# Graph layers on one core: the first chunk's turned tiles parked on chip, and five single operations moved

## The chip, the cores and the metric

One core of a Trainium2 chip runs the whole program. The metric is the device time of one execution in microseconds (us), from launch to end. Engines are named as in the profile: PE (TensorE, matmuls), DVE (VectorE), ACT (ScalarE), POOL (GpSimd), SP (SyncE). DMA queues are named by the engine that issues into them.

## The reference, cut to what matters

`adj` is 4096 x 4096 in float32 (sparse, random weights), `x` is 4096 x 128. Four layers run one after another; each is `x = layernorm(x + layer(x))`:

```python
# layer 0: two products with adj
out = adj @ (sum(d_list * filt * d_list)[:, None] * (adj @ (x @ weight))) + bias
# layer 1: A' = a * A, with (1 - a) added on the diagonal
out = relu((A' @ x) / rowsum(A') [:, None] @ W.T + b)
# layer 2: lap_mul(A, x) = d * (A @ (d * x)), d = 1 / sqrt(rowsum(A))
z = leaky_relu(lap_mul(A, x) @ W1 + b1, 0.1)
S = exp(-sqrt(max(|z_i - z_j|^2, 0) + 1e-10) / 2), kept for the 4 nearest j of each row, else 0
out = lap_mul(S + A, x) @ W2 + b2
# layer 3
out = relu(concat([x, A @ x]) @ W.T + b)
```

The program needs five products with `adj`. Every one goes over all of `adj`, so the transposed matrix is made once and read again.

## The kernel before

**Pass 0.** `adj` comes in 8 chunks of 512 rows. SP loads a chunk in 512-column units into four `nat` buffers in `region`. For each of the chunk's 32 tiles (`kt`) PE transposes four 128 x 128 blocks into `pt` (L1330). ACT writes the high fp16 part of the turned tile (`split_high`, L671), DVE the low part (L1082), and both also sum rows (L682, L1094). Between the transposes PE does three matmuls (L1310, L1312, L1314) of the tile four earlier; every fp32-like product is three fp16 matmuls. While it does chunk 0, DVE builds the operand `yop` as well (L1041).

Tiles `kt < 7` (KEPT) of every chunk stay on chip, in `kept[c]`. The other 25 tiles of a chunk form 5 units of 5. A unit is written into one of two stages, alternately (`s = (5 * c + u) % 2`), and POOL writes the stage to `at_scratch` in HBM in two parts, of 3 and 2 tiles, 768 and 512 KB (`store_units`, L506). ACT may overwrite a stage's part only when its last store has landed (`stage_stored`), which is two units later. One queue, POOL's, carries these stores in the order in which they are issued; SP's queue carries the loads. Chunks 0 and 1 are written out in the program, the later ones run in a loop, in which a nop stands ahead of each store to hold the wait.

**Passes 1 to 3** read the units back (SP, `early_slot` first) and use the kept tiles from chip.

**Near phase** (layer 2's neighbours). For each of 32 blocks of rows `i`, PE makes 128 x 4096 closeness values in eight PSUM banks (L1419 to L1426; four by `first_banks`, four by `second_banks`). ACT copies the banks to `region` (L718), DVE finds the largest (MAX8, L1145) and their places (L1146). `PROJECTION_AT` places the steps of another small task in this stream: each `projection_step(k)` is, on PE, a projection of group k-1 (L1238) and a turn of group k (L1209), on ACT the two copies behind them. Key 2i-1 puts a step between the banks of row i, key 2i behind them. After every fourth row come POOL's distances and degree sums, ACT's Sqrt and Exp (`weights`), ACT's Sqrt of the degrees (L742), and DVE's `inverse(g)` (reciprocal L1151, product with a constant L1152), whose results feed POOL's `scales` and ACT's `high_y`.

**Pass 4** follows with 128 gathers by POOL (L605). **Pass 5** starts while layer 2's last part (`mix`, layernorm, `yop` at L880) is still running on DVE: it takes units u = 0 to 4 in turn, and `KEPT5[u]` are the kept columns, which are ready early, that PE does before unit u. The last chunk of pass 5 is done in two halves of 256 rows: `sums_half` on ACT, `project_half` on PE (into `late_nat`), `last_half` on DVE, the output store by ACT.

Of the kernel before, what the change touches and what calls it, by code (L numbers as in the profile page):

```python
# [25 lines left out]
ALU = mybir.AluOpType  # L26
# [14 lines left out]
X_PARTS = 8  # L41
TOP = 4
# [13 lines left out]
PROJECTION_AT = {1: 1, 2: 2, 4: 3, 5: 4, 7: 5, 8: 6, 10: 7, 11: 8}  # L56
# [23 lines left out]
def gnn_kernel(nc, x, adj, d_list, w0, filt, bias0, alpha, w1, b1, wz, bz, w2, b2, w3, b3, out):  # L80
# [19 lines left out]
    with ExitStack() as ctx:  # L100
# [10 lines left out]
        kept = sb("kept", [P, NCH, KEPT, 2, CHUNK], F16)  # L111
        slot_elems = UNIT * 2 * CHUNK
# [134 lines left out]
        stage_used = sem("stage_used")  # L247
# [137 lines left out]
        def _(sp):  # L385
# [20 lines left out]
            def early_slot(u):  # L406
# [6 lines left out]
                if u == UPC - 1:  # L413
                    sp.wait_ge(acc_full, NCH)
                for s in range(2):
                    units = NCH * UPC // 2 if u >= UPC - 2 + s else (UPC + 1 - s) // 2
                    for part in range(len(STORES)):
                        sp.wait_ge(stage_stored[s][part], 16 * units)
# [66 lines left out]
        def _(pool):  # L485
# [13 lines left out]
            def store_units(c, par, m):  # L499
                for u in range(UPC):  # L500
                    s = (par * UPC + u) % 2
                    for part, (k0, k1) in enumerate(STORES):
                        pool.wait_ge(low_done, c * KT + KEPT + u * UNIT + k1)
                        pool.nop(nofuse=True)
                        cols = slice(k0 * 2 * CHUNK, k1 * 2 * CHUNK)
                        pool.dma_start(at_dram[bass.ds(c, 1), u, :, cols].rearrange("c p n -> (c p) n"),  # L506
                                       stage_flat[s][:, cols]).then_inc(stage_stored[s][part], 16)
            each_chunk(pool, store_units)
# [77 lines left out]
            def scales(g_tiles, g):  # L586
                nc.gpsimd.tensor_tensor(S[:, g_tiles, :], S[:, g_tiles, :], dinv2y[:, g_tiles].unsqueeze(2)
# [59 lines left out]
        def _(act):  # L647
# [5 lines left out]
            def split_high(c, par, m):  # L653
                for kt in range(KT):
                    g = c * KT + kt
                    act.wait_ge(tr_done, g + 1)
                    if kt < KEPT:
                        dst = kept[:, bass.ds(c, 1), kt, 0, :].rearrange("p c n -> p (c n)")
                    else:
                        u = (kt - KEPT) // UNIT  # L660
                        s = (par * UPC + u) % 2
                        if (kt - KEPT) % UNIT == 0 and not (isinstance(c, int) and c * UPC + u < 2):
# [4 lines left out]
                        for part, (k0, k1) in enumerate(STORES):  # L667
                            if (kt - KEPT) % UNIT == k0 and not (isinstance(c, int) and c * UPC + u < 2):
                                act.wait_ge(stage_stored[s][part], 16 * (m * UPC + (par * UPC + u) // 2))
# [25 lines left out]
            each_chunk(act, split_high, 4)  # L695
# [36 lines left out]
            def weights(g):  # L732
# [4 lines left out]
                nc.scalar.activation(S[:, tiles_g, :], S[:, tiles_g, :], ACT.Exp, scale=-0.5).then_inc(S_ready, 1)  # L737

# [36 lines left out]
            projection_step(0)  # L775
# [75 lines left out]
        def _(dve):  # L851
# [158 lines left out]
            def last_half(h):  # L1010
# [7 lines left out]
                dve.wait_ge(x3_loaded[(NCH - 1) % X3_BUFFERS], 16 * ((NCH - 1) // X3_BUFFERS + 1))  # L1018
                step(nc.vector.scalar_tensor_tensor(t_nat[:, half, :], t_nat[:, half, :], 0.0,
                                                    gath[(NCH - 1) % X3_BUFFERS][:, half, :], ALU.max, ALU.add))  # L1020
# [51 lines left out]
            def split_low(c, par, m):  # L1072
                for kt in range(KT):
                    g = c * KT + kt
                    dve.wait_ge(high_done, g + 1)
                    if kt < KEPT:
                        hi = kept[:, bass.ds(c, 1), kt, 0, :].rearrange("p c n -> p (c n)")
                        lo = kept[:, bass.ds(c, 1), kt, 1, :].rearrange("p c n -> p (c n)")
                    else:
# [570 lines left out]
```

## Time and profile before

| | us |
|---|---|
| median of 3 runs | 1424.22 |
| lowest, highest | 1420.53, 1425.78 |
| the profiled execution, its own time | 1423.97 |
| its span, first to last instruction | 1422.4 |

The granted clock of PE is 0.999 of full speed over the span. The profiled execution stands 0.25 us under the median; 1.57 us of its time lie outside the span. A busy share of an engine is an average over stages: pass 0 (to about 400 us), the streaming passes (to about 840), the near phase (to about 1140), pass 4 with its gathers, and pass 5.

### The profile page before, as it was taken

Reading aid. Unit: us, or ns where it says so; the run is one execution under the profiler, and the core shown is the slowest. Engines: PE = TensorE matmul, PEld = TensorE weight load, DVE = VectorE, ACT = ScalarE, POOL = GpSimd, SP = SyncE. Lnnn points to the kernel's source line nnn. Section 1 sums busy time; section 2 is a strip of 40 time slices with the busy share of each in tenths; the row PEclk is TensorE's granted clock in tenths of the full one; section 3 lists DMA queues with packets and bytes.
Section 4 is the critical chain, followed back from the end, with each engine's and each line's share of the span. In section 5 each row is a group of like instructions: output and inputs, shape, how many; then the busy total and the mean of one; then the engine's idle time right before and its main releaser. Section 6 shows DMA issues by size and latency. Waiting matters only on the chain.

```text
span 1422.4 us, 20428 instructions
## 1 busy us (share of the span) xinstructions
PE 1385.7 (97%) x7365; PEld 794.7 (56%) x7365; DVE 849.1 (60%) x1324; ACT 452.7 (32%) x958; POOL 236.0 (17%) x356
## 2 busy tenths in 40 slices
PE   7999999999999999999999999999999999999998
PEld 6888887877544444544445445444444444444467
DVE  7877766666323433434323359999999846655144
ACT  5767665655300000000010136655555410000011
POOL 2111110110100100000000000111111167776000
PEclk9999999999999999999999999999999999999999
DMA  9999998887999879987787812203444699999863
GB/s 348 393 376 386 357 329 327 319 301 268 335 388 355 348 303 391 412 356 297 291 325 277 307 31 89 89 16 119 133 134 133 237 391 403 404 379 403 353 244 115
DMA packets 111699, 407.53 MB, mean 287 GB/s; under 512 B 11696, under 2 KB 28080, under 8 KB 90112
## 3 DMA queue, kind: packets, MB, share of 16 engines
q1 hardware_dynamic: 79520, 316.43, 59.9%
q0 software_dynamic: 19728, 73.71, 13.3%
q10 hardware_dynamic: 12368, 16.26, 3.2%
q8 instruction: 55, 0.90, 0.2%
q14 instruction: 28, 0.23, 0.0%
HBM read 339.77 MB, written 66.58 MB: 286 GB/s over the span
## 4 chain that ended last, share of the span: by engine, by line
PE 66%; DVE 19%; DMA 7%; POOL 4%; issue 2%; ACT 1%; SPq 0%; DVEq 0%; POOLq 0%; ACTq 0%
PE acc L1262 10%; PE acc L1264 10%; PE acc L1263 10%; DVE hT L1145 8%; PE pt L1330 5%; DVE wT L1146 4%; DMA region<-in_adj 4%; POOL gath_all L605 4%; DVE wz_sb L1146 3%; PE pt L1264 3%; PE pt L1262 3%; PE pt L1263 3%; PE acc L1310 3%; PE acc L1312 2%; PE acc L1314 2%
## 5 line engine op out<-in xcount | busy, mean ns | idle before, releaser
L1330 PE MATMUL pt<-ident,region 128*128 128x128 f32 x1024 | 244.0, 279 | 13.5 <-DMA region<-in_adj 12.6
L1330 PEld LDWEIGHTS pt<-ident,region 128*128 128x128 f32 x1024 | 200.4, 196 | 40.8 <-issue 7.7
L1262 PE MATMUL acc<-region,yop 128*128 128x512 f16 (+1 forms) x581 | 217.8, 375 | 4.0 <-DVE yop L880 2.7
L1264 PE MATMUL acc<-region,yop 128*128 128x512 f16 (+1 forms) x581 | 217.5, 374 | 0.0
L1263 PE MATMUL acc<-region,yop 128*128 128x512 f16 (+1 forms) x581 | 217.5, 374 | 0.0
L1082 DVE SCALAR_TENSOR_TENSOR region<-pt,region 128x512 f16<-128x512 f32 x200 | 136.2, 687 | 75.5 <-ACT region L671 74.9
L718 ACT ACTIVATE region<-pt 128x512 f32<-128x512 f32 x256 | 133.0, 603 | 114.5 <-PE pt L1426 46.4
L671 ACT ACTIVATE region<-pt 128x512 f16<-128x512 f32 x200 | 118.1, 596 | 110.1 <-PE pt L1330 99.6
L1145 DVE MAX8 hT<-region 128x8 f32<-128x4096 f32 x31 | 136.8, 4412 | 2.3 <-ACT region L718 2.3
L1419 PE MATMUL pt<-yop 128*128 128x512 f16 x256 | 97.9, 382 | 8.6 <-ACT region L718 7.5
L639 ACT ACTIVATE std<-mv,eps_ln 128x4 f32<-128x4 f32 x31 | 9.2, 297 | 280.0 <-DVE mv L889 280.0
L1420 PE MATMUL pt<-yop 128*128 128x512 f16 x256 | 97.0, 379 | 0.0
L1421 PE MATMUL pt<-yop 128*128 128x512 f16 x256 | 97.0, 379 | 0.0
L1262 PEld LDWEIGHTS acc<-region,yop 128*128 128x128 f16 x581 | 56.8, 98 | 70.6 <-issue 6.0
L1262 PE MATMUL pt<-region,yop 128*128 128x512 f16 x250 | 94.8, 379 | 1.5 <-DMA region<-at_scratch 1.5
L1263 PE MATMUL pt<-region,yop 128*128 128x512 f16 x250 | 94.8, 379 | 0.0
L1264 PE MATMUL pt<-region,yop 128*128 128x512 f16 x250 | 94.8, 379 | 0.0
L506 POOL DMA_DIRECT2D at_scratch<-region x80 | 42.6, 532 | 308.6 <-DVE region L1082 298.9
L1264 PEld LDWEIGHTS acc<-region,yop 128*128 128x128 f16 x581 | 56.9, 98 | 65.9
L1263 PEld LDWEIGHTS acc<-region,yop 128*128 128x128 f16 x581 | 56.9, 98 | 59.8
L1094 DVE TENSOR_REDUCE rs_part<-region 128x1 f32<-128x512 f32 x128 | 86.6, 676 | 0.0
L1310 PE MATMUL acc<-region,yop 128*128 128x512 f16 x200 | 75.8, 379 | 2.5 <-DVE yop L1041 2.5
(257 smaller groups left out, 2278.8 us busy)
## 6 DMA issues: line engine op xcount, KB each, us to landing
region<-at_scratch SPq DMA_DIRECT2D x163, 1280.0 KB, 8.0
region<-in_adj SPq DMA_DIRECT2D x128, 512.0 KB, 7.6
at_scratch<-region POOLq DMA_DIRECT2D x40, 768.0 KB, 6.7
at_scratch<-region POOLq DMA_DIRECT2D x40, 512.0 KB, 6.8
region<-at_scratch SPq DMA_DIRECT2D x76, 256.0 KB, 2.7
x_scratch<-xout ACTq DMA_DIRECT2D x16, 256.0 KB, 10.8
region<-at_scratch ACTq DMA_DIRECT2D x3, 1280.0 KB, 9.8
gath_all<-x_scratch POOLq DMA_DIRECT2D x12, 256.0 KB, 5.3
```

Of the source, the lines that this page charges most:

```text
L671: nc.scalar.activation(dst, pt[kt % 4][:, :], ACT.Copy, scale=A_SCALE).then_inc(high_done, 1)
L718: nc.scalar.activation(near[i % 2][:, j * CHUNK:(j + 1) * CHUNK], near_bank(i, j)[:, :], ACT.Copy).then_inc(near_copied, 1)
L1082: nc.vector.scalar_tensor_tensor(lo, pt[kt % 4][:, :], A_SCALE, hi, ALU.mult, ALU.subtract).then_inc(low_done, 1)
L1145: step(nc.vector.max(top8[:, i, :], near[i % 2]))
L1146: nc.vector.max_index(idx8(i), top8[:, i, :], near[i % 2]).then_inc(near_used, 1)
L1262: nc.tensor.matmul(into, y[:, 0, kt, :], high, start=(kt == first_tile), stop=False)
L1263: nc.tensor.matmul(into, y[:, 0, kt, :], low, start=False, stop=False)
L1264: return nc.tensor.matmul(into, y[:, 1, kt, :], high, start=False, stop=(kt == last_tile))
L1310: nc.tensor.matmul(acc[par][:, :], yh, hi, start=(kt == 0), stop=False)
L1330: ins = nc.tensor.transpose(pt[kt % 4][:, t * P:(t + 1) * P], nat[u % 4][:, t, b * BLOCK + j:(b + 1) * BLOCK:PAIR], ident[:, :])
L1419: nc.tensor.matmul(into, zh, zT[:, 0, cols], start=True, stop=False)
L1420: nc.tensor.matmul(into, zh, zT[:, 1, cols], start=False, stop=False)
```

## The change

The 25 tiles of chunk 0 that are not kept go into the kept store of chunks 4 to 7, which is empty so far (`parked`), and not into the stages. POOL writes each parked unit to HBM later, as one transfer of 128 x 5120 fp16 (1.31 MB), behind the store of another chunk's unit: `PARKED_AT` says that unit 0 goes behind unit 2 of chunk 2, unit 1 behind (3, 1), unit 2 behind (4, 1), units 3 and 4 behind (5, 0) and (5, 2). ACT waits for them at the start of chunks 4, 5 and 6 (`PARKED_BEFORE`). ACT's and POOL's loops over the chunks are written out, and the nop ahead of a store is gone. The five moves: the projection steps are placed anew, with step 0 behind row 1; the product with a constant leaves `inverse` for POOL's `scales`; ACT does a Sqrt of one column behind the last Exp; the last chunk's bias is added by a PE matmul (identity by bias, 128 x 256 in f32) and no longer by DVE, and ACT's `sums_half(1)` stands behind the first half's output; one column of KEPT5 moves from unit 4 to unit 1.

```diff
+PARKED = 4
+PARKED_AT = {(2, 2): 0, (3, 1): 1, (4, 1): 2, (5, 0): 3, (5, 2): 4}
+PARKED_BEFORE = {4: 2, 5: 3, 6: 5}
...
-PROJECTION_AT = {1: 1, 2: 2, 4: 3, 5: 4, 7: 5, 8: 6, 10: 7, 11: 8}
+PROJECTION_AT = {2: 0, 3: 1, 4: 2, 6: 3, 7: 4, 8: 5, 10: 6, 11: 7, 12: 8}
...
+        def parked(k0, k1):
+            return kept_tiles[:, PARKED * KEPT + k0 - KEPT:PARKED * KEPT + k1 - KEPT, :, :]
...
+                sp.wait_ge(parked_stored, 16 * UPC)
...
-            def store_units(c, par, m):
+            for c in range(1, NCH):
                 for u in range(UPC):
-                    s = (par * UPC + u) % 2
+                    s = (c * UPC + u) % 2
                     for part, (k0, k1) in enumerate(STORES):
                         pool.wait_ge(low_done, c * KT + KEPT + u * UNIT + k1)
-                        pool.nop(nofuse=True)
...
+                    if (c, u) in PARKED_AT:
+                        k = PARKED_AT[c, u]
+                        pool.dma_start(at_dram[0, k, :, :], parked(KEPT + k * UNIT, KEPT + (k + 1) * UNIT)
+                                       .rearrange("p k h n -> p (k h n)")).then_inc(parked_stored, 16)
...
+                step(nc.gpsimd.tensor_scalar(dinv2y[:, g_tiles], dinv2[:, g_tiles], 1.0 / Y_SCALE[3], None, ALU.mult))
...
+                    if kt == 0 and c in PARKED_BEFORE:
+                        act.wait_ge(parked_stored, 16 * PARKED_BEFORE[c])
...
+                    elif c == 0:
+                        dst = parked(kt, kt + 1)[:, 0, 0, :]
...
-            each_chunk(act, split_high, 4)
+            for c in range(NCH):
+                split_high(c, c % 2, c // 2)
...
+                if g == NCH - 1:
+                    nc.scalar.activation(std[:, 0:1], eps_ln[:, 0:1], ACT.Sqrt)
...
-            sums_half(1)
             for h in range(2):
                 half = slice(h * TPC // 2, (h + 1) * TPC // 2)
+                if h == 1:
+                    sums_half(1)
...
-                nc.vector.tensor_tensor(t_nat[:, half, :], late_nat[:, half, :], bias[5][:, :].unsqueeze(1).to_broadcast([P, TPC // 2, D]),
-                                        ALU.add).then_inc(nat_read, 1)
+                dve.wait_ge(x3_loaded[(NCH - 1) % X3_BUFFERS], 16 * ((NCH - 1) // X3_BUFFERS + 1))
+                nc.vector.scalar_tensor_tensor(t_nat[:, half, :], late_nat[:, half, :], 0.0,
+                                               gath[(NCH - 1) % X3_BUFFERS][:, half, :], ALU.max, ALU.add
+                                               ).then_inc(nat_read, 1)
...
-                step(nc.vector.reciprocal(dinv2[:, g_tiles], droot[:, g_tiles]))
-                nc.vector.tensor_scalar(dinv2y[:, g_tiles], dinv2[:, g_tiles], 1.0 / Y_SCALE[3], None, ALU.mult
-                                        ).then_inc(dinv_ready, 1)
+                nc.vector.reciprocal(dinv2[:, g_tiles], droot[:, g_tiles]).then_inc(dinv_ready, 1)
...
-            KEPT5 = [[0], [1], [2], [3], [4, 5], [6]]
+            KEPT5 = [[0], [1, 2], [3], [4], [5], [6]]
...
-                pe.wait_ge(hT_ready, n)
...
+                nc.tensor.matmul(late_nat[:, half[0]:half[-1] + 1, :], ident[:, :],
+                                 bias[5][:, :].unsqueeze(1).to_broadcast([P, TPC // 2, D]), start=True, stop=False)
+                for t in half:
+                    nc.tensor.matmul(late_nat[:, t, :], xT[:, t * P:(t + 1) * P], wT[:, 1, :], start=False, stop=False)
+                pe.wait_ge(hT_ready, n)
+                for t in half:
+                    last = nc.tensor.matmul(late_nat[:, t, :], hT[:, t * P:(t + 1) * P], wT[:, 2, :], start=False, stop=t == half[-1])
```

On POOL, pass 0, in the loop of the kernel before (`region` holds the stages; the ISA rows are the nops with the wait):

```order
L506 ISA
L506 DMA at_scratch<-region 128x3072
L503 REGISTER_ALU
L506 ISA
L506 DMA at_scratch<-region 128x2048
L503 REGISTER_ALU
```

The same place in the changed kernel, chunk 3, units 1 and 2 (`kept` holds the parked unit):

```order
L514 DMA at_scratch<-region 128x3072
L514 DMA at_scratch<-region 128x2048
L517 DMA at_scratch<-kept 128x5120
L514 DMA at_scratch<-region 128x3072
L514 DMA at_scratch<-region 128x2048
```

The parked unit's transfer, which waits for nothing, stands in POOL's queue between the stores of units 1 and 2; the waits for DVE's low part are on the stores themselves.

On PE, near phase, the kernel before, from the middle of row 1 (its first banks end with the first row, `yop` is the operand of the closeness):

```order
L1426 MATMUL pt<-gath_all,ones 128x512 x4
L1238 MATMUL acc<-w_sb,xT 128x128 x4
L1209 MATMUL acc<-ident,t_nat 128x128 x4
L1419 MATMUL pt<-yop 128x512
L1420 MATMUL pt<-yop 128x512
```

The same in the changed kernel, from the middle of row 1 on (L1438 is the first matmul of a bank's three, L1445 its last):

```order
L1445 MATMUL pt<-gath_all,ones 128x512 x4
L1438 MATMUL pt<-yop 128x512
L1439 MATMUL pt<-yop 128x512
...
L1445 MATMUL pt<-gath_all,ones 128x512 x4
L1226 MATMUL acc<-ident,t_nat 128x128 x4
L1438 MATMUL pt<-yop 128x512
```

The projection and the turn between the halves of row 1 are gone; behind row 1 stands the turn of step 0, which stood ahead of row 1.

## Rows read from the trace of the kernel before

**Rows 1.** The page, part 1: busy time of each engine over the span.

```profile
PE 1385.7 (97%) x7365; PEld 794.7 (56%) x7365; DVE 849.1 (60%) x1324; ACT 452.7 (32%) x958; POOL 236.0 (17%) x356
```

**Rows 2.** Windows: us, busy of PE, PEld, DVE, ACT, POOL; clock, DMA share, GB/s.

```profile
14.00:51.00 37.00, 32.57 (x200) 28.22 (x199) 34.34 (x62) 24.02 (x56) 10.32 (x19) 1.00 1.04 393
...
205.00:220.00 15.00, 13.69 (x87) 11.83 (x86) 11.81 (x21) 10.83 (x27) 2.13 (x4) 1.00 1.02 400
```

**Rows 3.** Timeline, ACT and DVE in chunk 0: start, us, operation, [idle before].

```profile
30.26 0.60 ACT L671 ACTIVATE region<-pt 128x512 f16<-128x512 f32 x1 [1.71 <-DMA at_scratch<-region]
...
46.51 0.69 DVE L1082 SCALAR_TENSOR_TENSOR region<-pt,region 128x512 f16<-128x512 f32 x1 [0.73 <-ACT region L671]
```

**Rows 4.** Timeline, ACT and PE late in chunks 3 and 4.

```profile
165.66 0.60 ACT L671 ACTIVATE region<-pt 128x512 f16<-128x512 f32 x1 [2.17 <-PE pt L1330]
...
169.12 0.38 PE L1330 MATMUL pt<-ident,region 128*128 128x128 f32 x1 [0.73 <-DMA region<-in_adj]
...
210.28 0.60 ACT L671 ACTIVATE region<-pt 128x512 f16<-128x512 f32 x1 [2.11 <-DMA at_scratch<-region]
...
218.80 0.39 PE L1330 MATMUL pt<-ident,region 128*128 128x128 f32 x1 [1.31 <-DMA region<-in_adj]
```

**Rows 5.** DMA from 150 to 170 us, POOL's queue: packets, MB, share of 16 engines.

```profile
q0 software_dynamic: 895, 4.06, 50.5%
```

**Rows 6.** Timeline, PE, ACT and DVE at the start of the near phase.

```profile
845.11 0.65 PE L1209 MATMUL acc<-ident,t_nat 128*128 128x128 f32 x4
...
848.61 1.16 PE L1238 MATMUL acc<-w_sb,xT 128*128 128x128 f32 x8
...
848.71 2.07 ACT L718 ACTIVATE region<-pt 128x512 f32<-128x512 f32 x4 [2.31 <-PE pt L1426]
...
850.04 0.38 PE L1419 MATMUL pt<-yop 128*128 128x512 f16 x1
...
855.25 4.43 DVE L1145 MAX8 hT<-region 128x8 f32<-128x4096 f32 x1 [2.31 <-ACT region L718]
...
857.65 2.07 ACT L718 ACTIVATE region<-pt 128x512 f32<-128x512 f32 x4 [1.46 <-PE pt L1426]
...
858.31 0.41 PE L1419 MATMUL pt<-yop 128*128 128x512 f16 x1 [0.74 <-ACT region L718]
```

**Rows 7.** Timeline, DVE at the first inverse.

```profile
891.92 0.18 DVE L1151 RECIPROCAL inv_deg<-dinv 128x4 f32<-128x4 f32 x1 [1.14 <-ACT dinv L742]
892.14 0.17 DVE L1152 TENSOR_SCALAR scale<-inv_deg 128x4 f32<-128x4 f32 x1
892.22 4.42 DVE L1145 MAX8 hT<-region 128x8 f32<-128x4096 f32 x1
```

**Rows 8.** POOL's waits, 1130 to 1160 us: us in total, times, longest.

```profile
POOL gath_all L605 <- DMA y_scratch<-region: 5.5, 1, 5.5
```

**Rows 9.** Timeline, ACT behind the last Exp of the near phase.

```profile
1136.01 1.28 ACT L742 ACT_TABLE_LOAD   x1
1137.30 0.21 ACT L742 ACTIVATE dinv<-dinv 128x4 f32<-128x4 f32 x1
```

**Rows 10.** Timeline, PE and DVE in pass 5, around its unit 1.

```profile
1253.05 0.38 PE L1262 MATMUL acc<-kept,yop 128*128 128x512 f16 x1
...
1256.72 0.38 PE L1264 MATMUL pt<-kept,yop 128*128 128x512 f16 x1
1259.79 0.39 PE L1262 MATMUL acc<-region,yop 128*128 128x512 f16 x1 [2.69 <-DVE yop L880]
...
1279.34 0.69 DVE L880 SCALAR_TENSOR_TENSOR yop<-xout,yop 128x512 f16<-128x512 f32 x1
```

**Rows 11.** Timeline, PE and DVE at the end, second half of the last chunk.

```profile
1416.13 0.49 PE L1590 MATMUL pt<-wT,xT 128*128 128x128 f32 x2 [0.47 <-ACT hT L827]
...
1417.32 0.42 DVE L1015 TENSOR_TENSOR t_nat<-pt,bias 128x256 f32<-128x256 f32 x1 [0.23 <-PE pt L1591]
1417.78 0.43 DVE L1019 SCALAR_TENSOR_TENSOR t_nat<-t_nat,gath_all 128x256 f32<-128x256 f32 x1
```

More of the change, by code:

```diff
@@ L111, in gnn_kernel @@
         kept = sb("kept", [P, NCH, KEPT, 2, CHUNK], F16)
+        kept_tiles = kept[:, :, :, :, :].rearrange("p c k h n -> p (c k) h n")
+        def parked(k0, k1):
+            return kept_tiles[:, PARKED * KEPT + k0 - KEPT:PARKED * KEPT + k1 - KEPT, :, :]
         slot_elems = UNIT * 2 * CHUNK
@@ L414, in early_slot @@
                     sp.wait_ge(acc_full, NCH)
+                sp.wait_ge(parked_stored, 16 * UPC)
                 for s in range(2):
-                    units = NCH * UPC // 2 if u >= UPC - 2 + s else (UPC + 1 - s) // 2
-                    for part in range(len(STORES)):
-                        sp.wait_ge(stage_stored[s][part], 16 * units)
+                    if u >= UPC - 2 + s:
+                        for part in range(len(STORES)):
+                            sp.wait_ge(stage_stored[s][part], 16 * (NCH * UPC // 2 - (UPC + 1 - s) // 2))
             for k, (c, u, k0) in enumerate(UNITS1):
@@ L661, in split_high @@
                         s = (par * UPC + u) % 2
-                        if (kt - KEPT) % UNIT == 0 and not (isinstance(c, int) and c * UPC + u < 2):
+                        if (kt - KEPT) % UNIT == 0 and c * UPC + u >= UPC + 2:
                             if u == 1:
@@ L667, in split_high @@
                         for part, (k0, k1) in enumerate(STORES):
-                            if (kt - KEPT) % UNIT == k0 and not (isinstance(c, int) and c * UPC + u < 2):
-                                act.wait_ge(stage_stored[s][part], 16 * (m * UPC + (par * UPC + u) // 2))
+                            if (kt - KEPT) % UNIT == k0 and c * UPC + u >= UPC + 2:
+                                act.wait_ge(stage_stored[s][part], 16 * ((c * UPC + u) // 2 - (UPC + 1 - s) // 2))
                         dst = stage[s][:, (kt - KEPT) % UNIT, 0, :]
@@ L1078, in split_low @@
                         lo = kept[:, bass.ds(c, 1), kt, 1, :].rearrange("p c n -> p (c n)")
+                    elif isinstance(c, int) and c == 0:
+                        hi, lo = (parked(kt, kt + 1)[:, 0, h, :] for h in range(2))
                     else:
@@ L1286, in stored @@
                     return [kept[:, bass.ds(c, 1), kt, h, :].rearrange("p c n -> p (c n)") for h in range(2)]
+                if c == 0:
+                    return [parked(kt, kt + 1)[:, 0, h, :] for h in range(2)]
                 s = (par * UPC + (kt - KEPT) // UNIT) % 2
@@ L1585, in project_half @@
                 n = nth(ALL, 5, NCH - 1) + h
-                pe.wait_ge(hT_ready, n)
                 pe.wait_ge(xT_ready, nth(XTS, 5, NCH - 1))
                 pe.wait_ge(nat_read, n - 1)
-                for t in range(TPC)[h * TPC // 2:(h + 1) * TPC // 2]:
-                    nc.tensor.matmul(late_nat[:, t, :], xT[:, t * P:(t + 1) * P], wT[:, 1, :], start=True, stop=False)
-                    last = nc.tensor.matmul(late_nat[:, t, :], hT[:, t * P:(t + 1) * P], wT[:, 2, :], start=False, stop=True)
+                half = range(TPC)[h * TPC // 2:(h + 1) * TPC // 2]
+                nc.tensor.matmul(late_nat[:, half[0]:half[-1] + 1, :], ident[:, :],
[5 more added lines that the diff above has]
+                    last = nc.tensor.matmul(late_nat[:, t, :], hT[:, t * P:(t + 1) * P], wT[:, 2, :], start=False, stop=t == half[-1])
                 last.then_inc(nat_full, 1)
```

13 lines of the change are left out of this document (3 added, 10 removed).

## The prediction

> **What bounds the kernel now.** I read the page first, part 1: PE is busy for 1385.7 of 1422.4 us [rows 1]. Only 36.7 us of the span are PE's idle time, so an edit helps only where PE waits, or where the stage is another engine's. Then I asked, stretch by stretch, what PE waits for, and took the windows of the stretches that have idle time.
>
> In chunk 0 of pass 0 (14 to 51 us) PE is busy for 32.57 of 37.00 us, DVE for 34.34, and the DMA engines are full, share 1.04 at 393 GB/s [rows 2]: DVE is nearest to its limit, and PE follows it. ACT waits there 1.71 us for a stage's store, and later DVE 0.73 us for ACT [rows 3]. In chunks 1 to 7 PE sets the pace. Its idle time there is small; what of it this change can touch sits late in chunks 3 and 4: 0.73 and 1.31 us, both for loads of `adj` [rows 4]. Just ahead of each, ACT waits for over 2 us [rows 4], and in 205 to 220 us the DMA engines are full again, share 1.02 at 400 GB/s [rows 2]. PE's idle time in that window, 15.00 - 13.69 = 1.31 us, is that one wait.
>
> In the near phase DVE is the bound: its MAX8 and FIND_INDEX8 follow each other without a gap, and the timeline shows a 2.31 us hole only ahead of row 1 and 1.14 us ahead of the first inverse [rows 6, 7]. In pass 5 PE is the bound again, with one hole, 2.69 us, before unit 1 [rows 10]. At the end a short chain runs PE, DVE, ACT, output [rows 11].
>
> **Parking, what it takes away.** Ten stores (five units, 6.55 MB) leave chunk 0. DVE has 37.00 - 34.34 = 2.66 us to give back there, so the gain lies between 0 and 2.66. ACT's wait of 1.71 for a store does not appear as such on DVE; what DVE shows as its own is 0.73 [rows 3]. I take 0.7 us.
>
> **Parking, what it adds.** Five transfers of 1.31 MB in POOL's queue. At the 400 GB/s of the full stretch one takes 1.31 / 0.400 = 3.3 us. If the load queue goes on taking its half, the store queue has 4.06 MB in 20 us [rows 5], that is 0.203 MB/us, and one takes 6.5 us. If it falls where the DMA engines have room, it costs nothing. So each lies between 0 and 6.5 us, and what matters is who waits behind it. The parked units behind (2, 2), (5, 0) and (5, 2): the stage that (2, 3) fills is not needed again before the seven kept tiles of the next chunk have passed, in which nothing is stored; chunk 5 shows no load wait on PE in the list of its waits. I take 0 for these three (both bounds kept). The units behind (3, 1) and (4, 1) stand in the queue ahead of the store of unit 2. Unit 4 needs that stage, at the 28th tile, where ACT already waits 2.17 and 2.11 us [rows 4]. Behind this wait of ACT stand its copies out of `pt`, then DVE's low part, then PE's transposes, as `pt` has four buffers. A store that lands 3.3 us later makes ACT wait 3.3 us longer. PE paid 0.73 for ACT's 2.17 and 1.31 for 2.11, one third to six tenths, and the slack of the buffers is used. I take 0.55 of it, 1.8 us in each of chunks 3 and 4. Together 3.6 us, with bounds 0 and 2 x 6.5 = 13.
>
> The Trainium skill, page "DMA: Bandwidth & Descriptors", section "Queues, rings and completion order", says that each DMA engine takes a queue's descriptors in the order of its ring; it speaks against this change, since a parked transfer then delays every store behind it. Its section "Bandwidth" (where the 436 GB/s come from) holds that traffic between HBM and on-chip memory is bound near 358 GB/s for a core. By that a parked unit takes 1.31 / 0.358 = 3.7 us (an estimate) and the sum comes out 0.4 us higher; the trace's 393 and 400 GB/s lie above that figure, so the measurement decides.
>
> The new waits at the starts of chunks 4, 5 and 6 stand on ACT ahead of the chunk's first tile, with DVE's and PE's work behind them. They ask for units issued at least two units of another chunk earlier; the landing that I fear above is some 10 us, so they cost nothing unless the queue is that far behind. The same holds for SP's wait before pass 1: the last parked unit is issued in chunk 5. Loops written out and nops dropped: no row prices them. They can at most take away the 0.73 + 1.31 us of rows 4; I take 0 and keep 2.0 for the range.
>
> **Projection steps.** Between the halves of row 1 PE does L1238 and L1209 from 848.61 to 850.04, that is 1.43 us, and only then the second banks [rows 6]. Without them the second banks start when the first bank is copied out: in row 2 that is 858.31 - 857.65 = 0.66 us behind ACT's first copy. In row 1 ACT starts at 848.71, so 849.37, a gain of 0.67. The turn that stood ahead of row 1 (845.11, 0.5 us) is gone as well, so ACT can start up to 0.5 us sooner: 1.16 at most from there. I take 1.0; the hole of 2.31 us is the upper bound, 0 the lower. Row 2 now has a step between its halves, 1.43 us, but DVE spends about 8.9 us on a row (855.25 to the next MAX8), which covers it.
>
> **Inverse without the product.** From the reciprocal to MAX8 DVE needs 892.22 - 891.92 = 0.30 us [rows 7]. With the reciprocal alone I take the 0.1 us that lie between its neighbours' starts at least (892.14 to 892.22 is 0.08), so 0.2 is saved. It stands eight times, seven of them between searches: 1.4 us (0 to 7 x 0.22 = 1.5). POOL gets an operation of some 0.2 us ahead of `scales`; before the gathers POOL waits 5.5 us for a DMA [rows 8], which covers it; uncovered it would cost 0.2 once.
>
> **The extra Sqrt.** The table load at 1136.01 is followed by the Sqrt of the degrees 0.01 us after its end, 1136.01 + 1.28 = 1137.29 [rows 9]. The load already starts behind the Exp; the extra Sqrt only puts an operation of some 0.2 us between. The last inverse's shorter DVE work gives that back. I take 0, from -0.2 to 0.2; if the load had been held by the wait for the degrees, 1.28 would be gained, but the row shows it started ahead.
>
> **KEPT5.** PE ends column 1 at 1256.72 + 0.22 and starts unit 1 at 1259.79, when DVE's `yop` is there [rows 10]: 2.85 us lost. A kept column takes 1256.94 - 1253.05 = 3.89 us, more than the hole. Column 2 fills it, unit 1 starts at 1260.8, and unit 4 later has one column less ahead of it. Unit 2's `yop` is ready at 1279.34 + 0.69 = 1280.0; unit 2 starts at about 1260.8 + 6 x 3.89 = 1284.1, so no new hole. Gain 2.9 (0 to 2.9).
>
> **The end.** L1238's eight instructions are four f32 matmuls of 128 x 128 in 1.00 us, 0.25 each; the bias matmul of 128 x 256 is bounded by 0.25 and 1.0, taken as 0.5. In the first half PE is busy throughout: +0.5. In the second, bias and x part (1.0) start in PE's hole of 0.47 us [rows 11], so the h part comes 0.53 later than `hT` and takes 0.5, against 1.0 of both parts before: +0.03. DVE has one operation less, 1417.78 - 1417.32 = 0.46. Together 0.1, taken as 0, from -0.5 to +1.0. `sums_half(1)` behind the first half's output changes only output that is early; cost 0, at most the 0.23 us by which DVE waits.
>
> **Sum**, against the profiled execution's own 1423.97 (0.25 below the median): -0.7 -1.0 -1.4 -2.9 +3.6 = -2.4, so 1421.6.
>
> **Rivals.** *Parking is hidden* (B): the full stretches have just room for a parked unit, or `pt` and the load buffers absorb it. For it: PE's own loss in chunks 3 and 4 is short. Against: shares of 1.02. Time 1423.97 - 6.0 = 1418.0, and 1415.9 if the waits of rows 4 go too. *The small moves give nothing* (C): each hole is only moved, to row 2, to the next inverse, to unit 2. For it: engines stand close behind each other there; against: the 4 us that unit 2 has, and DVE's 8.9 us a row. Time 1423.97 - 0.7 + 3.6 = 1426.9. *The store queue falls behind* (D, slower): each parked unit delays all stores behind it by 6.5 us and PE pays it whole. Two such: 1418.0 + 13.0 = 1431.0; with (2, 2) as a third, 1437.5. It decides once parking costs over 13.1 us, since about 0.5% of 1424.2, 7.1 us, is what a measurement of this kernel can tell from no change. For it: the share of 50.5% in rows 5, and the ring order named above. Against: the loads catch up in every chunk's kept stretch.
>
> **Chances.** My forecast 0.56, B 0.27, C 0.11, D 0.06. The likeliest's own range is 1418 to 1425. B's lower half, and some of the first with more gain in chunk 0, lie under 1417.1: faster 0.25. D's upper part is slower, 0.06. The rest is same, 0.69. Range 1414.5 to 1428: it takes in B and C, and leaves out D and the sum of all best bounds.
>
> **What would show it.** The hole before unit 1 is gone, unit 1 at 1260.8 less what was gained before; the wait ahead of row 1's MAX8 is 1.3 in place of 2.31; reciprocal to MAX8 0.1. In chunk 0 ACT has no wait for a store. Late in chunks 3 and 4 ACT's wait is about 3 us longer and PE's near 2.5 to 3.1. If PE's idle time there is not above rows 4, B was right; if chunk 5, or the waits at the starts of chunks, show PE idle, D. The prediction is wrong if chunk 1 changes its pace, which I hold equal.

## The result, and the profile after

The changed kernel takes 1432.49 us (median of 6 runs, 1431.42 to 1437.02), the kernel before 1424.52 us in the runs beside it (1420.53 to 1426.11). The ratio is 1.0052, with a 95% interval of 1.0034 to 1.0069: it is slower by half a percent. The forecast was 1421.6 us, range 1414.5 to 1428. The profiled execution of the changed kernel took 1432.9 us, 8.9 more than that of the kernel before.

I read the new trace in three steps: where on the time axis the two executions part, what PE waits for there, and what the DMA queues do meanwhile. For the first step I took, from the timelines of DVE, the start of the low part of tile 8 of each chunk in both kernels. Their difference, changed minus before, is in us:

| chunk | 1 | 2 | 3 | 4 | 5 | 6 | 7 | end of pass 0 | row 1's MAX8 | last reciprocal | last output store |
|---|---|---|---|---|---|---|---|---|---|---|---|
| changed - before | -0.8 | -2.0 | +5.3 | +10.7 | +13.8 | +15.0 | +15.1 | +15.1 | +13.3 | +11.8 | +8.8 |

So the change gains 2.0 us up to chunk 2, loses 17 us in chunks 2 to 6, and gains 6.2 us back behind pass 0. The waits of PE from 9 to 420 us (line waited for, us in total, times, longest), first of the kernel before:

```profile
PE pt L1330 <- DMA region<-in_adj: 5.2, 5, 1.6
PE pt L1330 <- DVE region L1082: 0.8, 2, 0.5
```

and of the changed kernel:

```profile
PE pt L1349 <- DMA region<-in_adj: 11.5, 6, 4.9
PE pt L1349 <- DVE region L1101: 3.4, 2, 2.3
```

PE's waits for loads and for the low part grow from 6.0 to 14.9 us over the pass. Some of the old ones, in chunks 0 and 1, are gone or shorter; in the stretch that loses the 17 us, from tile 8 of chunk 2 to tile 8 of chunk 6, they grow from 2.8 to 14.3 us, by 11.5. The rest is in PE's busy time of the same stretch, first before, then changed (columns as in [rows 2]; third from the end is PE's clock):

```profile
101.11:277.57 176.46, 173.51 (x1061) 143.60 (x1060) 127.97 (x209) 113.90 (x264) 21.27 (x40) 1.00 0.94 346
99.12:292.62 193.50, 179.19 (x1061) 145.23 (x1060) 128.29 (x209) 114.96 (x264) 23.88 (x45) 0.96 0.93 350
```

The same 1061 matmuls take 5.7 us longer, and the mean clock is 0.96. So 11.5 us of the 17 are waits and 5.7 are slower matmuls. Here are the waits on PE's timeline in the changed kernel, with two product matmuls behind the longest:

```profile
125.21 0.39 PE L1349 MATMUL pt<-ident,region 128*128 128x128 f32 x1 [1.26 <-DMA region<-in_adj]
...
134.75 0.49 PE L1349 MATMUL pt<-ident,region 128*128 128x128 f32 x1 [4.91 <-DMA region<-in_adj]
135.03 0.63 PE L1319 MATMUL pxT<-kept,yop 128*128 128x512 f16 x1
...
138.18 0.38 PE L1319 MATMUL pxT<-kept,yop 128*128 128x512 f16 x1
...
174.29 0.39 PE L1349 MATMUL pt<-ident,region 128*128 128x128 f32 x1 [2.26 <-DVE region L1101]
...
177.56 0.49 PE L1349 MATMUL pt<-ident,region 128*128 128x128 f32 x1 [1.82 <-DMA region<-in_adj]
...
223.72 0.39 PE L1349 MATMUL pt<-ident,region 128*128 128x128 f32 x1 [1.16 <-DVE region L1101]
...
226.68 0.48 PE L1349 MATMUL pt<-ident,region 128*128 128x128 f32 x1 [1.60 <-DMA region<-in_adj]
...
282.98 0.38 PE L1349 MATMUL pt<-ident,region 128*128 128x128 f32 x1 [1.30 <-DMA region<-in_adj]
```

The row at 134.75 is at the start of chunk 3, in its kept stretch. The matmul behind it lasts 0.63 us, three microseconds later the same one lasts 0.38. The windows of the changed kernel show why:

```profile
130.00:135.00 5.00, 0.25 (x1) 0.22 (x2) 1.45 (x3) 1.08 (x3) 0.00 (x0) 0.95 1.03 413
135.00:140.00 5.00, 5.00 (x22) 3.04 (x21) 0.96 (x2) 0.60 (x1) 0.00 (x0) 0.71 1.05 404
175.00:180.00 5.00, 3.18 (x13) 1.93 (x13) 3.43 (x7) 2.78 (x8) 1.06 (x2) 0.54 1.03 397
180.00:185.00 5.00, 5.00 (x25) 3.66 (x24) 2.83 (x5) 2.94 (x7) 0.00 (x0) 0.77 1.04 405
225.00:230.00 5.00, 3.40 (x12) 2.15 (x12) 2.95 (x7) 2.80 (x8) 1.06 (x2) 0.66 1.04 404
```

Behind three of the waits the granted clock falls from 2.4 to 1.2 GHz and comes back some us later; before, no window of pass 0 shows less than 1.00. The deficits add up to 5 x (0.05 + 0.29 + 0.46 + 0.23 + 0.34) = 6.9 us; that is at most what the clock adds to the waits, since PE also idles in part of it, and it agrees with the 5.7 us by which the busy time grew.

What the DMA engines do while the first parked unit moves is in the queue view from 122 to 126 us (packets, MB, share of 16 engines; q0 is POOL's queue, q1 SP's with the loads). The kernel before:

```profile
q0 software_dynamic: 227, 0.94, 56.8%
q1 hardware_dynamic: 371, 0.72, 46.2%
```

The changed kernel:

```profile
q0 software_dynamic: 160, 1.33, 78.9%
q1 hardware_dynamic: 161, 0.32, 20.8%
```

160 packets of stores stand against 161 of loads. Before the change the counts are not equal, because POOL's queue ran low within these 4 us (37 packets beside 152 from 124 to 125 us; 70 beside 74 from 123 to 124, while it was full). While both queues have work, the engines take one packet of each in turn, and a packet of POOL's queue has 8.3 KB in the mean (1.33 MB / 160), one of the loads 2 KB. The loads get 0.32 MB in 4 us, 80 GB/s, less than half of what they had. The Trainium skill tells of these turns on its page "DMA: Bandwidth & Descriptors", section "Queues, rings and completion order": an engine goes round its queues packet by packet. The trace agrees, with its 160 to 161. Of that section I had used only the order within a queue.

Two of the five moves can be read off DVE's timeline, as forecast. The hole before row 1's MAX8 is 1.30 us, where it was 2.31, and MAX8 stands 0.09 us behind the reciprocal, where it was 0.30 [rows 6, 7]:

```profile
868.53 4.43 DVE L1164 MAX8 hT<-region 128x8 f32<-128x4096 f32 x1 [1.30 <-ACT region L734]
...
905.20 0.18 DVE L1170 RECIPROCAL inv_deg<-dinv 128x4 f32<-128x4 f32 x1 [1.15 <-ACT dinv L760]
905.29 4.40 DVE L1164 MAX8 hT<-region 128x8 f32<-128x4096 f32 x1
```

### The profile page after: what moved, and what is told of

Same layout as the page of the kernel before. It is cut to its first block, busy times and chain, and to the rows that moved or that the text cites. A ratio compares the mean times of both kernels' runs of the same rounds, so it can differ in the third digit from the quotient of the medians.

```text
span 1431.2 us, 19922 instructions
## 1 busy us (share of the span) xinstructions
PE 1390.1 (97%) x7369; PEld 796.8 (56%) x7369; DVE 846.4 (59%) x1314; ACT 453.9 (32%) x959; POOL 237.4 (17%) x359
## 4 chain that ended last, share of the span: by engine, by line
PE 73%; DVE 18%; DMA 7%; ACT 1%; issue 1%; SPq 0%; DVEq 0%
PE acc L1279 10%; PE acc L1280 10%; PE acc L1281 10%; DVE hT L1164 8%; PE pt L1349 5%; DMA region<-in_adj 5%; PE pt L1279 5%; PE pt L1281 5%; PE pt L1280 5%; DVE wT L1165 4%; DVE wz_sb L1165 3%; PE acc L1329 3%; PE acc L1331 3%; PE acc L1333 3%; PE pnat L1246 2%; DMA region<-at_scratch 1%
## 5 line engine op out<-in xcount | busy, mean ns | idle before, releaser
L1349 PEld LDWEIGHTS pt<-ident,region 128*128 128x128 f32 x1024 | 200.9, 196 | 50.9 <-DMA region<-in_adj 13.3
L1101 DVE SCALAR_TENSOR_TENSOR region<-pt,region 128x512 f16<-128x512 f32 x175 | 118.9, 687 | 74.9 <-ACT region L686 74.7
L686 ACT ACTIVATE region<-pt 128x512 f16<-128x512 f32 x175 | 103.4, 595 | 99.2 <-PE pt L1349 87.7
L1438 PE MATMUL pt<-yop 128*128 128x512 f16 x256 | 98.0, 383 | 5.8 <-ACT region L734 4.2
L514 POOL DMA_DIRECT2D at_scratch<-region x70 | 37.2, 532 | 325.4 <-DVE region L1101 325.4
L1101 DVE SCALAR_TENSOR_TENSOR kept<-pt,kept 128x512 f32 (+1 forms) x81 | 55.2, 686 | 41.1 <-ACT kept L686 41.0
```

Of the source, the lines that this page charges most:

```text
L686: nc.scalar.activation(dst, pt[kt % 4][:, :], ACT.Copy, scale=A_SCALE).then_inc(high_done, 1)
L1101: nc.vector.scalar_tensor_tensor(lo, pt[kt % 4][:, :], A_SCALE, hi, ALU.mult, ALU.subtract).then_inc(low_done, 1)
L1349: ins = nc.tensor.transpose(pt[kt % 4][:, t * P:(t + 1) * P], nat[u % 4][:, t, b * BLOCK + j:(b + 1) * BLOCK:PAIR], ident[:, :])
L1438: nc.tensor.matmul(into, zh, zT[:, 0, cols], start=True, stop=False)
```

## The experiments

The theory that I took into them: the parked transfers starve the loads of `adj`, PE waits, and its clock falls behind the longest waits. The rivals: the written-out loops disturb pass 0; or it is the new waits and what chunk 0 does with the kept store; or each byte costs the same wherever it is written; or packets have nothing to do with it. All comparisons with "before" are with runs on the same chip. Two experiments set against each other may come from different chips, on which the kernel before takes 1424.5 to 1427.9 us in the median, so such a difference is good to two or three us only. The ratio is an estimate of its own from the runs, with its 95% interval; it differs from the quotient of the two medians by up to 0.001.

**The moves without the parking.**

```diff
-            for c in range(1, NCH):
+            for c in range(NCH):
...
-                    elif c == 0:
-                        dst = parked(kt, kt + 1)[:, 0, 0, :]
```

> The changed kernel with its parking undone: chunk 0's units go through the stages and are written in chunk 0 as before; the five moves and the written-out loops without nops stay. Theory (parked transfers starve the loads of adj, PE waits, and its clock falls after the longest waits): pass 0 ends as early as in the kernel before, within 1 us, no stretch at a clock of 0.5, and the moves keep their worth of about 6 us: 1417 to 1420 us. Rival (the written-out loops, with stores issued sooner, disturb pass 0): PE still waits 5 us or more in chunks 3 and 4 and the time is 1426 or more.

Measured: 1414.22 us against 1425.87, ratio 0.9909 (0.9892 to 0.9926). There is no clock below 1.00 in pass 0, which ends 3.8 us earlier than before. PE's waits for loads from 9 to 420 us:

```profile
PE pt L1342 <- DMA region<-in_adj: 2.6, 5, 0.8
```

The loops are not the cause of the loss. The time is below what I expected, and it is the best of all kernels here. Against the changed kernel, 18 us are the parking's by the medians, 20 by the two ratios.

**The parking without the moves.**

```diff
-            KEPT5 = [[0], [1, 2], [3], [4], [5], [6]]
+            KEPT5 = [[0], [1], [2], [3], [4, 5], [6]]
...
+            projection_step(0)
```

> The changed kernel with its five moves undone; the parking and the written-out loops stay. Theory: pass 0 ends some 15 us later than before, and nothing is given back after it: 1437 to 1440 us. Rival (the moves bring a loss or nothing, pass 0's loss is partly theirs): 1431 to 1434.

Measured: 1437.46 us, ratio 1.0071 (1.0050 to 1.0092). Pass 0 ends 13.2 us late. The theory holds: the moves have no part in the loss.

**The same transfers in the kept stretches.** POOL waits for the seventh kept tile of chunks 1 to 5 and writes a parked unit then.

```diff
+                if c in PARKED_AT:
+                    k = PARKED_AT[c]
+                    pool.wait_ge(low_done, c * KT + KEPT)
+                    pool.dma_start(at_dram[0, k, :, :], parked(KEPT + k * UNIT, KEPT + (k + 1) * UNIT)
+                                   .rearrange("p k h n -> p (k h n)")).then_inc(parked_stored, 16)
                 for u in range(UPC):
```

> The changed kernel, but the parked units are issued in chunks 1 to 5, each when the chunk's seven kept tiles are done and ahead of the store of unit 0, where the DMA engines of the kernel before have room (shares of 0.66 to 0.9). Theory (the place decides, since a parked transfer hurts where the engines are full): PE's waits for loads in chunks 3 to 6 fall back to those of the kernel before (3 us or less together), no clock of 0.5, the gain of chunks 0 to 1 of about 1 us stays: 1415 to 1419. Rival (each 1.31 MB costs its time wherever it stands): PE still loses 10 us or more, 1427 or more.

Measured: 1417.81 us, ratio 0.9935 (0.9917 to 0.9953). The place decides most of it: 14.7 us less than the changed kernel with the same bytes and packets, and no clock of 0.5 in pass 0. But it stays 3.6 us behind the kernel without parking, and pass 0 ends 1.3 us later than before, not earlier (in the profiled execution, the slowest of the six with 1420.56). Parking brings nothing even here.

**Smaller packets.**

```diff
+                        for t in range(UNIT):
+                            pool.dma_start(at_dram[0, k, :, t * 2 * CHUNK:(t + 1) * 2 * CHUNK],
+                                           parked(KEPT + k * UNIT + t, KEPT + k * UNIT + t + 1)
+                                           .rearrange("p k h n -> p (k h n)")).then_inc(parked_stored, 16)
```

> The changed kernel, but each parked unit is written as five transfers of one tile, 2 KB a row in place of 10 KB, at the same places. Theory with turns by packet (the engines alternate between the queues packet by packet, so a 10 KB packet leaves a 2 KB load a sixth of the time): while a parked unit moves the loads carry about half the bytes in place of a fifth; PE's longest wait falls from 4.9 to 3 us or less, 1424 to 1429 us. Rival (only the bytes in POOL's queue count): waits as in the changed kernel, 1430 to 1434.

Measured: 1427.14 us, ratio 1.0004 (0.9992 to 1.0017), 5.3 less than the changed kernel. PE's longest wait is 3.94 us in place of 4.91, where I had expected 3 at most. The queues from 122 to 126 us in this kernel:

```profile
q0 software_dynamic: 316, 1.03, 63.7%
q1 hardware_dynamic: 319, 0.62, 39.9%
```

Again one packet of each in turn, 316 to 319. The packets of the parked tiles hold 4 KB, not the 2 KB of a row that I had counted on, so the loads get 0.62 of 1.65 MB and not the half that I expected; it is twice what they had in the changed kernel. The turn by packet is shown in these counts. Smaller packets take back about a third of the loss; the rest remains with them.

**The loops alone.**

```diff
-                        pool.nop(nofuse=True)
...
-            each_chunk(pool, store_units)
...
-            each_chunk(act, split_high, 4)
+            for c in range(NCH):
+                split_high(c, c % 2, c // 2)
```

> The kernel before with only ACT's and POOL's loops over the chunks written out and the nops ahead of the stores gone: no parking, none of the five moves. In the kernel with the moves alone pass 0 ended 3.8 us earlier than in the kernel before, which no move touches. Theory (it is the sooner issue of the stores): pass 0 ends 3 to 4 us earlier here too, 1420 to 1422.5 us against some 1425 on the same chip. Rival (that difference was one execution's chance): within 1 us of the kernel before.

Measured: 1423.49 us, ratio 0.9987 (0.9978 to 0.9996). Pass 0 ends 2.3 us earlier, the time is 1.5 us less, both under what I expected. In the profiled execution part of what pass 0 gained was lost again in pass 5, told in the last section.

**One tile behind each unit.**

```diff
+                    k, t = divmod((c - 1) * UPC + u, UNIT)
+                    if k < UPC:
+                        pool.dma_start(at_dram[0, k, :, t * 2 * CHUNK:(t + 1) * 2 * CHUNK],
+                                       parked(KEPT + k * UNIT + t, KEPT + k * UNIT + t + 1)
+                                       .rearrange("p k h n -> p (k h n)")).then_inc(parked_stored, 16)
```

> The changed kernel, but the 25 parked tiles are written one at a time, 256 KB each, behind each of the 25 units of chunks 1 to 5. The bytes are the same. Theory (a large transfer of large packets in a full stretch starves the loads; a small one is made up before PE notices): no clock of 0.5, PE's waits for loads after the first 3 to 6 us together, 1417 to 1421 us. Rival (every parked byte in chunks 1 to 5 costs alike): as with 4 KB packets, about 1427.

Measured: 1429.56 us, ratio 1.0037 (1.0024 to 1.0051). This expectation fell, and with it the idea that a small transfer is made up before PE notices. PE waits for loads again at the starts of chunks 2 and 3:

```profile
94.44 0.39 PE L1350 MATMUL pt<-ident,region 128*128 128x128 f32 x1 [2.86 <-DMA region<-in_adj]
...
133.18 0.49 PE L1350 MATMUL pt<-ident,region 128*128 128x128 f32 x1 [2.46 <-DMA region<-in_adj]
```

The clock falls behind both, to 0.66 in the window from 95 to 100 us and 0.80 in that from 130 to 135. The loss has come forward: the kernel is 4.5 us late in chunk 2 already, where the changed kernel is 2.0 early, and 8.2 in chunk 3. My reading is that what decides is how many bytes a chunk's full stretch gets; this run alone does not show it, the extra transfers late in the pass (below) test it. A chunk moves 4096 x 512 x 4 bytes of loads and 6.55 MB of stores, 14.9 MB, which is 37 us at the 405 GB/s of the full windows. By the starts of their first low parts in the trace of before, chunks 1, 2, 3, 4 and 5 last 38.1, 40.6, 41.9, 44.7 and 50.4 us. So chunk 1 has 1 us of room, chunk 2 has 4, chunk 3 has 5, and chunk 5 has 13; and the room lies at the chunk's start, in and behind the kept tiles, which are not written. 1.31 MB more are 3.2 us. The small figures are rough: counted from tile 8 to tile 8, chunk 1 has 3.5 us of room and chunk 2 has 2.4. The trace of the kernel before could have told it ahead, in the share of the DMA engines (second from the end) of chunks 1, 2 and 5, each from its tile 8 to the next chunk's:

```profile
60.62:101.11 40.49, 39.25 (x248) 34.26 (x247) 31.67 (x53) 27.87 (x66) 5.32 (x10) 1.00 1.00 378
101.11:140.56 39.45, 38.92 (x245) 33.50 (x244) 31.48 (x52) 28.16 (x66) 5.31 (x10) 1.00 1.01 381
228.44:277.57 49.13, 49.03 (x294) 38.67 (x293) 32.63 (x53) 28.96 (x66) 5.32 (x10) 1.00 0.88 311
```

Over the whole of chunks 1 and 2 the share is 1.00 and 1.01, close to the 1.03 to 1.05 of the full windows above; chunk 5 has room.

**One unit moved.**

```diff
-PARKED_AT = {(2, 2): 0, (3, 1): 1, (4, 1): 2, (5, 0): 3, (5, 2): 4}
+PARKED_AT = {(3, 1): 1, (4, 1): 2, (5, 0): 3, (5, 2): 4}
...
+                if c == 2:
+                    pool.wait_ge(low_done, c * KT + KEPT)
```

> The changed kernel with one parked unit moved: unit 0 is issued ahead of chunk 2's unit 0 instead of behind its unit 2. Theory (each parked unit's loss is its own, and unit 0's is the 8 us at the start of chunk 3): the wait of 4.9 us and the clock of 0.5 at 135 us are gone, those in chunks 3 and 4 stay; 1425 to 1428 us. Rival (the loads are late by then anyway and the loss turns up at the next full stretch): 1430 to 1433.

Measured: 1427.91 us, ratio 1.0015 (1.0004 to 1.0026). From chunk 2 to chunk 3 this kernel loses 3.0 us to the kernel before, where the changed kernel loses 7.3, and its clock is not reduced there; from chunk 3 to 5 it loses 9.2 us, the changed kernel 8.5. So moving unit 0 takes most of its loss away and leaves that of units 1 and 2 as it was: each unit's loss is its own.

**Transfers that nobody reads.**

```diff
+    more_dram = nc.dram_tensor("more_scratch", [UPC, P, UNIT * 2 * CHUNK], F16).ap()
...
+                        pool.dma_start(more_dram[k, :, :], kept[:, 1, 0:UNIT, :, :].rearrange("p k h n -> p (k h n)")).then_inc(parked_stored, 16)
```

> The kernel with the five moves and the written-out loops and no parking (1414.2 us), to which five transfers of 1.31 MB are added that nobody reads, from the kept tiles of chunk 1 to a scratch, at the five places of the parked ones. Chunk 0 writes its units itself, and ACT waits for no transfer at a chunk's start. Theory (the loss is the transfers' traffic at these places): 1431 to 1435 us, waits and clock as in the changed kernel. Rival (the loss comes from the new waits, or from what chunk 0 does with the kept store): below 1420.

Measured: 1432.78 us, ratio 1.0053 (1.0037 to 1.0068), 18.6 us above the kernel without them (which ran on another chip), and the same time as the changed kernel. PE waits where that one does:

```profile
136.72 0.49 PE L1343 MATMUL pt<-ident,region 128*128 128x128 f32 x1 [4.52 <-DMA region<-in_adj]
...
179.49 0.49 PE L1343 MATMUL pt<-ident,region 128*128 128x128 f32 x1 [1.75 <-DMA region<-in_adj]
```

So it is the traffic, at these places. The new waits on ACT and the use of the kept store cost nothing that can be measured, and taking ten stores out of chunk 0 brought next to nothing.

**KEPT5 as before.** The kernel of the moves without parking, with the old KEPT5.

```diff
-            KEPT5 = [[0], [1, 2], [3], [4], [5], [6]]
+            KEPT5 = [[0], [1], [2], [3], [4, 5], [6]]
```

> The kernel with the moves and without the parking (1414.2 us), with KEPT5 as in the kernel before. Theory (the hole before unit 1 costs its 2.7 to 3.2 us of waiting, and in those executions in which the clock falls to 0.5 behind it another 1.7): 1417.5 to 1419.5 us. Rival (only the wait counts): 1417 us at most, and no stretch at 0.5 near unit 1.

Measured: 1418.34 us, ratio 0.9951 (0.9936 to 0.9965), 4.1 us above the kernel with the new KEPT5. The profiled execution waits 3.47 us before unit 1 and shows no reduced clock there, which the loops-only kernel does show. The other executions have no trace, but their mean granted clock is on record: two executions at 1.000 took 1416.73 and 1416.98 us, two at 0.999 took 1418.34 and 1419.16, and one at 0.997 took 1420.74. Against 1414.22 the hole by itself then costs about 2.6 us, and executions with a lower clock lose more; that they lose it behind this hole is not shown.

**Stages tile by tile.**

```diff
+                        for t in range(k0, k1):
+                            cols = slice(t * 2 * CHUNK, (t + 1) * 2 * CHUNK)
+                            pool.dma_start(at_dram[c, u, :, cols], stage_flat[s][:, cols]).then_inc(stage_stored[s][part], 16)
```

> The kernel with the moves and without the parking, in which the stages go out tile by tile, 256 KB each, in place of 768 and 512 KB, issued when the part is done as now. Theory (smaller store packets leave the loads a larger share of the full stretches): PE's waits for loads after the first fall below the 2.5 us of that kernel, 1412 to 1414 us. Rival (the bytes count, not the packets): 1414 to 1416 us.

Measured: 1415.98 us, ratio 0.9932 (0.9918 to 0.9945). PE's waits for loads fall to 1.2 us, as the theory said, but the time is not lower than 1414.22 (the profiled execution is the slowest of the five, 1419.71). Where the bytes fit, smaller packets gain nothing here.

**Extra transfers late.**

```diff
-PARKED_AT = {(2, 2): 0, (3, 1): 1, (4, 1): 2, (5, 0): 3, (5, 2): 4}
+PARKED_AT = {(5, 0): 0, (5, 2): 1, (6, 0): 2, (6, 2): 3, (7, 0): 4}
```

> The kernel with the moves and without the parking, to which the same five transfers of 1.31 MB that nobody reads are added behind the units (5, 0), (5, 2), (6, 0), (6, 2) and (7, 0). Theory (a transfer costs where the chunk's bytes already fill its time: a chunk moves 14.9 MB, 37 us at 405 GB/s, and lasts 38 to 42 us in chunks 1 to 3 but 50 in chunks 5 to 7): 1414 to 1416.5 us, no clock of 0.5 in pass 0. Rival (a 10 KB packet starves the loads wherever it moves): 1420 or more.

Measured: 1415.12 us, ratio 0.9923 (0.9910 to 0.9937), 0.9 above the kernel without the transfers. The same five transfers of 10 KB rows that cost 18.6 us in chunks 2 to 5 cost about one in chunks 5 to 7. The profiled execution is the slowest of its five, 1418.53; it has one wait of 2.99 us at the start of chunk 6 with a fall of the clock behind it, which I had not expected. So the room of chunk 5 does not cover two units in every execution, and the room of a chunk is shown as what decides between the chunks tried here, not as an exact sum.

**The moves without the loops.** The kernel before with the five moves; the loops and nops stay as they were.

```diff
             each_chunk(pool, store_units)
...
             each_chunk(act, split_high, 4)
```

> The kernel before with the five moves alone: no parking, and ACT's and POOL's loops and the nops as they were. Theory (moves and loops add up: the loops alone gave 1.5 us, both together 11.6): some 10 us below the kernel before of the same chip, 1414.5 to 1417 us, and pass 0 within 1.5 us of the kernel before. Rival (the moves are worth the 5.3 us forecast, the loops the rest when they meet): 1419 to 1421 us.

Measured: 1417.01 us, ratio 0.9932 (0.9911 to 0.9953), 10.9 us below the kernel before. The profiled execution, 1416.76, is 7.2 below that of the kernel before, of which 1.0 is in pass 0. The moves and the loops add up, roughly.

## Why the prediction was wrong, step by step

**The step that failed is the term "what it adds" of the parking**: I took 3.6 us, and it is about 17. I asked who waits for the store queue, and followed only the stages. The loads of `adj` run on the same engines, and I priced what a parked unit does to them at nothing. I had even let the load queue keep its half while a parked unit moves; it kept 0.32 of 1.66 MB.

- Unit 0, behind (2, 2): taken as 0, because seven kept tiles cover the stage. From tile 0 to tile 8 of chunk 3 the changed kernel loses 8.0 us (from 2.7 early to 5.3 late), 4.91 of them in one wait for a load. The kept tiles cover the stage, but they are also the stretch in which the loads catch up.
- Units 1 and 2, behind (3, 1) and (4, 1): taken as 1.8 each. From chunk 3 to 4 the loss is 5.4 us, from chunk 4 to 5 it is 3.2. The wait that I had in view is there, in these rows of the changed kernel's ACT:

```profile
172.91 0.60 ACT L686 ACTIVATE region<-pt 128x512 f16<-128x512 f32 x1 [4.60 <-DMA at_scratch<-region]
...
222.34 0.60 ACT L686 ACTIVATE region<-pt 128x512 f16<-128x512 f32 x1 [3.51 <-DMA at_scratch<-region]
```

  In chunk 3 ACT waits 4.60 us for the store and PE 2.26 for DVE behind it, where I had forecast about 5 and 2.5; in chunk 4 they wait 3.51 and 1.16, where I had forecast about 5 and 3.1. To these come the loads' 1.82 and 1.60 us and the clock. One row under this term was misread: the 2.17 us of ACT at 165.66 [rows 4] ended with PE's transposes, not with a store; only the 2.11 at 210.28 is a wait for a store. So the "one third" that I took from the first has no row under it.
- Units 3 and 4: taken as 0; from chunk 5 to 6 the loss is 1.2 us.
- The clock had no term. It fell behind three waits, and the matmuls of chunks 2 to 6 took 5.7 us longer. Here an idle PE was paid twice, while it waited and behind it.

**What parking takes away** came out near the size taken, in part by luck: 0.7 us taken, 0.8 us measured by chunk 1. But the loops alone give 0.3 of that, and the kernel without parking reaches 0.2 by the same tile: less than 0.6 is left for parking. Chunk 0 gains next to nothing because DVE holds its pace, as read from [rows 2].

**The loops and nops** were taken as 0 with 2.0 as bound. They are worth 2.3 us of pass 0 in one profiled execution and 1.5 us of time; in the kernel with the moves pass 0 ends 3.8 us earlier, in the moves without loops 1.0. The time saved lies within the bound, though I took nothing of it; what pass 0 gains lies above the bound, so the two waits of rows 4 were no bound; where the rest comes from is not shown.

**The projection steps**: 1.0 taken, 2.31 - 1.30 = 1.01 measured. **The inverse**: 1.4 taken; from the first to the last reciprocal the lag falls from 13.3 to 11.8, 1.5. **The extra Sqrt**: 0 taken. In the changed kernel it stands 0.1 us ahead of the Sqrt of the degrees, behind the same table load of 1.28 us:

```profile
1147.72 1.28 ACT L755 ACT_TABLE_LOAD   x1
1149.01 0.20 ACT L755 ACTIVATE std<-eps_ln 128x1 f32<-128x1 f32 x1
1149.12 0.19 ACT L760 ACTIVATE dinv<-dinv 128x4 f32<-128x4 f32 x1
```

**KEPT5 and the end**: 2.9 taken. From the last reciprocal to the last output store the changed kernel gains 3.0 us, the kernel without parking 3.3, the moves without loops 3.9. The hole before unit 1 is gone: PE is busy for all of 1250 to 1275 us. In single profiled executions the moves are worth 6.0 to 6.2 us in all behind pass 0, against 5.3 taken; in medians on the same chip the moves alone are worth 10.9. Much of the gap goes with the clock. The profiled execution of the kernel before has a mean clock of 0.999; its eleven runs beside the moves alone have 0.997 in the mean, the six of the moves 0.9998. Time lost to the clock, one less the clock times the span, is then up to 4.6 us against 0.3, so about 4 of the 10.9 us. At which places those runs lost it no trace shows.

**The rivals.** D, "the store queue falls behind", put 1431.0 to 1437.5 on it and had 0.06. The time lies there, and POOL's queue is the place, but D had the later stores pay. They pay a part; the loads pay more. B (parking hidden) is refuted by the waits of chunks 3 and 4, and C by the moves' rows. Of the signs that I named, chunk 1 did change its pace: it gains 1.2 us (from 0.8 to 2.0 early). The kernel without parking gains 1.0 there, so this is not the parking's; it says that the loops and nops were worth more than nothing. PE idle at the starts of chunks was to speak for D by way of ACT's new waits at chunks 4 to 6; it came at the start of chunk 3, where no new wait stands, and for a load.

## What to carry to other kernels

Before transfers are moved into another stage, count all bytes of that stage against its time, loads included, and find in which part of it the room lies; a share under 1 over a whole pass says nothing of the stretch in which the transfer would stand. Here a store with large packets took its turns packet by packet beside the loads (160 to 161) and with them four fifths of the bytes, so those who wait for the other queue belong in the sum. A wait of PE of a few us in a stream of matmuls can bring a stretch at half clock behind it, so it can cost more than its length. Here the version that keeps the five moves and the written-out loops and leaves the parking out, 1414.22 us, beats both kernels.

## What the runs showed of the hardware that I had not expected

Idle PE, then half clock. In the loops-only kernel PE waits 3.21 us before unit 1 of pass 5 and starts again; about a microsecond later the matmuls start half as often:

```profile
1257.52 0.39 PE L1274 MATMUL acc<-region,yop 128*128 128x512 f16 x1 [3.21 <-DVE yop L892]
...
1258.63 0.63 PE L1276 MATMUL acc<-region,yop 128*128 128x512 f16 x1
1259.06 0.63 PE L1274 MATMUL acc<-region,yop 128*128 128x512 f16 x1
1259.49 0.63 PE L1275 MATMUL acc<-region,yop 128*128 128x512 f16 x1
...
1262.46 0.38 PE L1274 MATMUL acc<-region,yop 128*128 128x512 f16 x1
1262.67 0.38 PE L1275 MATMUL acc<-region,yop 128*128 128x512 f16 x1
```

The starts are 0.43 us apart at 1259 and 0.21 at 1262, and the windows of that kernel give a clock of 0.86 and 0.80 for 1255 to 1265 us:

```profile
1255.00:1260.00 5.00, 2.48 (x9) 1.04 (x10) 4.01 (x8) 0.00 (x0) 3.78 (x5) 0.86 1.01 395
1260.00:1265.00 5.00, 5.00 (x20) 2.04 (x19) 3.44 (x4) 0.00 (x0) 3.78 (x5) 0.80 0.54 156
```

That is 5 x (0.14 + 0.20) = 1.7 us lost behind a wait of 3.2. In the kernel before the same hole, 2.69 us [rows 10], had no such stretch behind it, nor had the one of 3.47 us with the old KEPT5. Whether the clock falls behind a wait is thus not told by the length of the wait alone.

Full DMA engines move more than the figure that I had weighed: the 122 to 126 us stretch carries 1.65 MB in 4 us before the change and 1.66 MB after it, 413 and 414 GB/s. The bound near 358 GB/s of the Trainium skill ("DMA: Bandwidth & Descriptors", section "Bandwidth") does not show here, where one core runs.
